# Rebuilding the two attentions of a two-layer kernel: paired maxima, single score banks, row sums inverted inside

## The reference

```python
x = L0_attn_x
xn = layernorm(x)
x = x + attn0(xn) + ternary_mlp(xn)      # attn0: 32 query heads of 16, 8 key heads, rope, causal softmax, wo
xn = layernorm(x)
x = x + gated_cumsum(xn) + attn1(xn)     # attn1: 16 heads of 32, causal softmax, Wp
# each attention: scores = q k^T * scale; softmax over the causal part; out = weight @ v; out @ w
```

## Time and profile before

| | |
|---|---|
| median of 3 runs | 3019.53 us (3016.12 to 3024.72) |
| profiled execution, its own time | 3012.14 us |
| its span | 3010.3 us |
| mean granted TensorE clock | 0.915 |
| TensorE busy (matmul) | 2623.4 us, 87% |
| VectorE busy | 1634.4 us, 54% |
| ScalarE busy | 1100.0 us, 37% |
| attention of layer 0 in the span, first load to last store | 554.1 to 1598.0 us |
| attention of layer 1, the same | 2155.8 to 2885.2 us |

### The profile page before, as it was taken

One profiled execution on the slowest core, in us unless ns is written; L12 is line 12 of the kernel. 1 busy time (PEld: TensorE's weight loads), 2 busy tenths in 40 slices (PEclk: granted clock), 3 DMA queues, 4 the chain that ended last, 5 costly groups with the idle time before them and its releaser, 6 DMA issues. The chain is left out here.

```text
span 3010.3 us, 38749 instructions
## 1 busy us (share of the span) xinstructions
PE 2623.4 (87%) x12386; PEld 1552.7 (52%) x12386; DVE 1634.4 (54%) x3332; ACT 1100.0 (37%) x1303; POOL 128.9 (4%) x84
## 2 busy tenths in 40 slices
PE   6969999589999999999995799797189999999945
PEld 3758888345555555555543577675144444444314
DVE  4644445587777777777712434311176665666313
ACT  2422222005565555555672222121014444444420
POOL 1200000300000000000000022100300000000000
PEclk8979999659999999999997899898569999999978
DMA  4741010401202202020003100252542122220023
GB/s 157 239 145 42 28 42 0 60 15 28 40 10 42 39 15 42 13 38 10 9 15 132 60 1 0 76 136 102 139 97 55 45 52 72 71 71 12 15 72 120
DMA packets 103924, 177.62 MB, mean 59 GB/s; under 512 B 39664, under 2 KB 45552, under 8 KB 97712
## 3 DMA queue, kind: packets, MB, share of 16 engines
q1 hardware_dynamic: 100272, 162.58, 20.7%
q10 hardware_dynamic: 3456, 12.58, 1.3%
HBM read 115.24 MB, written 59.90 MB: 58 GB/s over the span
## 5 line engine op out<-in xcount | busy, mean ns | idle before, releaser
L596 ACT ACTIVATE a_ex<-a_ps_s 128x1024 f32<-128x1024 f32 x960 | 832.6, 894 | 804.5 <-PE a_ps_s L668 404.1
L710 DVE TENSOR_REDUCE a_mx_part<-a_ps 128x1 f32<-128x512 f32 x1152 | 771.9, 688 | 255.0 <-PE a_ps L613 246.5
L613 PE MATMUL a_ps<-a_k,a_q 96*128 96x512 f32 (+3 forms) x1920 | 786.6, 452 | 97.4 <-DMA a_q<-q 92.8
L613 PEld LDWEIGHTS a_ps<-a_k,a_q 96*128 96x128 f32 x1920 | 369.5, 204 | 586.2 <-DVE a_mx_part L710 326.9
L635 PE MATMUL a_ps_o<-a_ex,a_v 128*32 128x512 f32 (+7 forms) x3840 | 607.6, 548 | 22.8 <-DVE a_o L735 19.1
L663 PE MATMUL a_ps_s<-a_q,a_k 128*128 128x512 f32 (+3 forms) x1920 | 607.6, 392 | 22.3 <-DMA a_q<-m_early 13.7
L706 DVE CUSTOM_DVE_ANT_0 a_junk<-a_ps,band 128x128 f32<-128x128 f32 (+3 forms) x768 | 369.3, 486 | 213.7 <-PE a_ps L613 210.5
L663 PEld LDWEIGHTS a_ps_s<-a_q,a_k 128*128 128x128 f32 x1920 | 353.4, 194 | 119.3 <-ACT a_ex L596 45.4
L635 PEld LDWEIGHTS a_ps_o<-a_ex,a_v 128*32 128x32 f32 (+1 forms) x3840 | 114.2, 117 | 212.9 <-issue 161.0
L668 PE MATMUL a_ps_s<-block_band,block_ident 128*128 128x128 bf16 x768 | 175.0, 234 | 0.0
L110 PE MATMUL w_ps<-w_oh,w_wh 128*128 128x512 f32 x128 | 54.7, 427 | 103.3 <-DVE w_ol L1042 103.3
(11 more groups left out here) (161 smaller groups left out, 2536.1 us busy)
## 6 DMA issues: line engine op xcount, KB each, us to landing
a_q<-q SPq DMA_DIRECT2D x48, 512.0 KB, 12.3
o<-a_o SPq DMA_DIRECT2D x64, 256.0 KB, 2.4
q<-p_oh SPq DMA_DIRECT2D x32, 256.0 KB
q<-p_ol SPq DMA_DIRECT2D x32, 256.0 KB
w_o<-o SPq DMA_DIRECT2D x32, 256.0 KB
w_z<-z SPq DMA_DIRECT2D x32, 256.0 KB
v<-p_v SPq DMA_DIRECT2D x32, 256.0 KB, 3.4
a_k<-k SPq DMA_DIRECT2D x8, 1024.0 KB, 8.4
```

What stands on the lines that cost most here:

```text
L596: act.activation(ex[unit % NE][:, :, off:CH], ps_s[unit % 2][:, :, off:CH], ACT.Exp, scale=SCALE).then_inc(exp_done, 1)
L613: pe.matmul(ps_1[bank][:, 0:w], q_st[set_][0:96, h, i * P:(i + 1) * P], k_st[set_][0:96, h % KH, kc * CH:kc * CH + w], start=True, stop=True)\
L710: dve.tensor_reduce(out, bank, AX.X, ALU.max).then_inc(taken1, 1)
```

## The change

What it does, part by part:

1. Pass 1 works on pairs of heads: two products into a pair of banks, and off the diagonal one VectorE reduction over both (128x2x512). Two pairs of banks take the place of three banks.
2. The score banks of pass 2 are three single ones, and exp works on one head at a time (1920 in place of 960). Six buffers `ex` instead of four.
3. Pass 1 runs `LEAD` = 21 steps ahead of pass 2 through all groups, not 40. Its rows are flipped per chunk, four times in a group.
4. The added mask product on the diagonal is f32r (`mask_sel`, `mask_low`, mask value -2^127), not bf16. Four constants are shaped on GpSimd one after another, two of them copied by DMA and all cast on VectorE before the first block ends.
5. The block `reciprocals` is gone. Inside the attention, SyncE reads the sums of each chunk back from DRAM (`load_sums`), VectorE inverts 128x16 or 128x8 of them (`invert`) and SyncE writes them (`store_sums`).
6. The chunk is copied out of PSUM by ScalarE (`stage`), not VectorE.
7. No loop: all groups are written out. No clearing of query and key tiles; the products take only the rows in use (48 or 96 in pass 1, 50 or 98 in pass 2), ones are set in 32 rows of the key tile.
8. `HALVES` is 1 for both attentions: all heads use rows from 0 on, and each head has a part of the query tile of its own.

The core of the diff, the new order of TensorE, SyncE and VectorE (constants, buffers and helpers that only change names are left out):

```diff
+LEAD = 21
+    FLIP_DELAY = 2 * PAIRS
+    FLIP_AT = {n + 1 + FLIP_DELAY: f for f, n in enumerate(sorted(LAST_BLOCK.values()))}
+    SLOTS = {s: range((s + LEAD) * PAIRS, (s + LEAD + 1) * PAIRS) for s in range(len(STEP_LIST))}
+    SLOTS[-1] = range(0, LEAD * PAIRS)
+    LAST_STEP = {s: (g, c) for s, (g, c, t) in enumerate(STEP_LIST) if t == TPC * c + TPC - 1}
...
         @block.sync
+            for g in range(2):
+                if ONES0 < KC:
+                    sp.wait_ge(blank, g + 1)
+                load(g)
+            for s in range(-1, len(STEP_LIST) + 8):
+                for n in SLOTS.get(s, ()):
+                    if n in FLIP_AT:
+                        put_rows(FLIP_AT[n], n)
+                if s >= 0 and s < len(STEP_LIST) and s % STEPS == 2 and s // STEPS + 2 < GROUPS:
+                    if s // STEPS > 0:
+                        sp.wait_ge(pv_done, s // STEPS * STEPS)
+                    elif ONES0 < KC:
+                        sp.wait_ge(blank, 3)
+                    load(s // STEPS + 2)
+                if s - 2 in LAST_STEP:
+                    store(*LAST_STEP[s - 2])
+                if s - 3 in LAST_STEP:
+                    load_sums(*LAST_STEP[s - 3])
+                if s - 6 in LAST_STEP:
+                    store_sums(*LAST_STEP[s - 6])
...
         @block.scalar
+            for s, (g, c, t) in enumerate(STEP_LIST):
+                if s - 2 in LAST_STEP:
+                    stage(*LAST_STEP[s - 2], s - 2)
+                for h in range(HG):
+                    act.wait_ge(scores2, n + 1)
+                    act.activation(ex[unit % NE][:, h % 2, off:CH], ps_s[n % 3][:, off:CH], ACT.Exp, scale=SCALE)\
+                        .then_inc(exp_done, 1)
...
         @block.tensor
+            for s, (g, c, t) in enumerate(STEP_LIST):
+                if t == 0:
+                    f = g * NCH + c
+                    pe.wait_ge(rows_in[f % 2], ROWS_IN * (f // 2 + 1))
+                for p in range(PAIRS):
+                    n = SLOTS[s][p]
+                    scores(s, 2 * p)
+                    if n in FLIP_AT:
+                        flip(n)
+                    if n < len(BLOCKS):
+                        max_scores(n)
+                    scores(s, 2 * p + 1)
+                if s > 0:
+                    times_v(s - 1)
...
         @block.vector
+            def invert(g, c):
+                j = g * NCH + c
+                dve.wait_ge(z_in[j % 2], 16 * (j // 2 + 1))
+                if j >= 2:
+                    dve.wait_ge(z_out[j % 2], 16 * (j // 2))
+                dve.reciprocal(zr[j % 2][:, :], z[j % 2][:, :]).then_inc(inverse, 1)
+            for s in range(-1, len(STEP_LIST) + 8):
+                for n in SLOTS.get(s, ()):
+                    if n in FLIP_AT:
+                        take_rows(n)
+                    if n < len(BLOCKS):
+                        maxima(n)
+                        g, i, kc, p = BLOCKS[n]
+                        if LAST_BLOCK[g, i // TPC] == n:
+                            whole_max(g, i // TPC, n)
+                if s - 5 in LAST_STEP:
+                    invert(*LAST_STEP[s - 5])
```

More of the change, by code:

```diff
@@ L443, in sem @@
         def sem(n):
[L445 to L451, removed]
+            return shared(f"at_{n}")
+        q_st = [sb(f"q{i}", [P, HG // HALVES, TOK], F32R) for i in range(NS)]
+        k_st = [sb(f"k{i}", [P, KH, TOK], F32R) for i in range(NS)]
+        v_st = [sb(f"v{i}", [P, VH, QT, VW]) for i in range(NS)]
@@ L452, in attention @@
         ex = [sb(f"ex{i}", [P, 2, CH]) for i in range(NE)]
         o_sb = [sb(f"o{i}", [P, CH]) for i in range(2)]
-        junk = [sb(f"junk{i}", [P, CH]) for i in range(NB)]
+        junk = [sb(f"junk{i}", [P, 2, CH]) for i in range(2)]
         mx_part = sb("mx_part", [P, HG, QT, NCH])
[L456 to L459, removed]
@@ L482, in attention @@
-        block = ctx.enter_context(nc.Block())
[L484 to L503, removed]
+        z_in = [sem(f"z_in{i}") for i in range(2)]
@@ L505, in _ @@
+        z_out = [sem(f"z_out{i}") for i in range(2)]
+        inverse = sem("inverse")
+        LOADS = (1 + 5 * HALVES) * 16
+        ROWS_IN = 16 * HALVES
+        block = ctx.enter_context(nc.Block())
         @block.sync
         def _(sp):
[L507 to L522, removed]
@@ L540, in store @@
-            def store(g, c):
[L541 to L565, removed]
@@ L568, in _ @@
             for b in range(2):
-                sp.wait_ge(stored[b], 16 * NCH // 2 * GROUPS + DMA0)
+                sp.wait_ge(stored[b], 16 * NCH * GROUPS // 2)
+                sp.wait_ge(z_out[b], 16 * NCH * GROUPS // 2)
         @block.gpsimd
         def _(pool):
[L573 to L580, removed]
+            for s in range(NS):
+                for e in range(HALVES):
+                    last = pool.memset(k_st[s][e * ROWS + ONES0:e * ROWS + ONES0 + 32].bitcast(F32), 1.0)
+                last.then_inc(blank, 1)
@@ L582, in _ @@
         @block.scalar
         def _(act):
[L584 to L590, removed]
-                    for pair in range(PAIRS):
-                        act.wait_ge(scores2, g * UNITS + unit + 1)
-                        if pair == 0:
-                            act.wait_ge(pv_done, g * STEPS + n + 1 - NE // PAIRS + PV0)
-                        act.activation(ex[unit % NE][:, :, off:CH], ps_s[unit % 2][:, :, off:CH], ACT.Exp,
-                                       scale=SCALE).then_inc(exp_done, 1)
-                        unit += 1
@@ L617, in flip @@
-            def flip(base, entry, count, early, first=False):
-                m = mx_early if early else mx_late
-                k = m.shape[1] * m.shape[2]
-                pe.wait_ge(part_max, count)
-                bank, before = bank1(entry, first)
-                pe.wait_ge(taken1, base + (before + 1))
-                pe.matmul(ps_1[bank][0:k, 0:P], m[:, :, :].rearrange("p h i -> p (h i)"),
+                if (i, kc, p) == (0, 0, 0):
+                    pe.wait_ge(landed[s], LOADS * (g // NS + 1))
@@ L712, in whole_max, with maxima @@
-            def whole_max(base, entry, early):
-                tiles = slice(0, EARLY_TILES) if early else slice(EARLY_TILES, QT)
-                dve.wait_ge(taken1, base + entry)
-                dve.tensor_reduce((mx_early if early else mx_late)[:, :, :], mx_part[:, :, tiles, :], AX.X, ALU.max)\
-                    .then_inc(part_max, 1)
-            def take_rows(base, entry, g, early, first=False):
-                n = 0 if early else 1
-                high, low = rows[early]
-                bank = ps_1[bank1(entry, first)[0]][0:high.shape[0], 0:P]
-                dve.wait_ge(scores1, base + (entry + 1))
-                if not isinstance(g, int) or g > 0 or not early:
-                    dve.wait_ge(rows_out[n], g * 32 + DMA0)
+            def maxima(n):
+                g, i, kc, p = BLOCKS[n]
+                m = entry(n)
+                w = min(CH, (i + 1) * P - kc * CH)
+                dve.wait_ge(scores1, m + 1)
+                bank = ps_1[m % 2]
+                if kc < i // TPC:
+                    dve.tensor_reduce(mx_part[:, 2 * p:2 * p + 2, i, kc], bank[:, :, 0:w], AX.X, ALU.max)\
+                        .then_inc(taken1, 1)
+                    return
+                for e in range(2):
+                    last = dve.tensor_tensor_reduce(out=junk[m % 2][:, e, 0:w], in0=bank[:, e, 0:w], in1=band[:, CH - w:CH],
+                                                    scale=1.0, scalar=NEG, op0=ALU.add, op1=ALU.max,
+                                                    accum_out=mx_part[:, 2 * p + e, i, kc:kc + 1])
+                last.then_inc(taken1, 1)
@@ new lines, in _ @@
+                pool.wait_ge(shaped, 3)
+                pool.affine_select(out=raw_low1[:, :], in_=raw_low1[:, :], compare_op=ALU.is_ge, fill=MASKED,
+                                   base=0, pattern=[[1, P]], channel_multiplier=-1).then_inc(shaped, 1)
+                pool.wait_ge(shaped, 4)
+                for part in range(2):
+                    pool.affine_select(out=raw_sel2[0:H, part, :], in_=raw_sel2[0:H, part, :], compare_op=ALU.not_equal,
+                                       fill=1.0, base=-1 - H * part, pattern=[[1, P]], channel_multiplier=-1)\
+                        .then_inc(shaped, 1)
+                    pool.wait_ge(shaped, 5 + part)
```

417 lines of the change are left out of this document (205 added, 212 removed).

## The result

The changed kernel took **3928.78 us** (median of 4 runs, 3926.66 to 3932.37) against 3021.23 for the kernel before, measured beside it: a ratio of 1.3007, 95% interval 1.2984 to 1.303. Forecast were 3086, with a range up to 3150. The sign was right. The size was not: some 840 us are missing from the sum, and no rival held them.

The account below looks back on a forecast made before the run. TensorE was taken to set the pace inside a group. Gains and costs summed to -89 us, the new wait added +155.5, so +66.5 on 3012.1, or 3086 us on the median; range 2985 to 3150.

Parts of the forecast that it names:

- the clearing at the start of layer 0: Layer 0's first load no longer waits for the clears, only one short memset is ahead of it: -8.8 us.
- the old 2.95 us per step: Layer 0's time per step with pass 1 beside pass 2, from the earlier profile: 117.9 us a group over 40 steps.
- The new wait: VectorE's inversion waits for sums read behind a load, stalling TensorE 10.0 and 13.6 us, five times per layer: +155.5 us.
- rival D: Chunk 3's rows, flipped in step 21, come late for step 24 in layer 1: 3096 to 3120 us, chance 0.10.
- rival A: The sums come in time, so the wait does not arise: 2930 us, faster than before, chance 0.20.
- rival B: The wait behind the load is there but half as long, +70 to +90: 3000 to 3020 us, chance 0.12.
- The sum without the wait: All priced parts of the change together, before the inversion's wait behind the load: -89 us.
- constants: Four more selects in a chain, a DMA and four casts before the first block: +5 us, bounds 3 and 8.
- wait for the copy-out: TensorE's 19.1 us of waiting for VectorE's copy in 42 places shrinks with ScalarE copying: -15 us, bounds 0 and -40.
- The term for the mask: Of 768 f32r mask products on the diagonal, 192 with 128 columns cost about 0.036 us more each: +7 us.
- The -2 for pairs of maxima: Pairing saves one of two VectorE reductions' start-up in 84 and 42 maxima of pass 1 alone: about -2 us.
- rival C: The f32r mask's weight loads are not hidden, +68 us on the forecast: 3150 us, chance 0.08.

Follow-up runs that it names:

- run 1: Changed kernel with layer 0's score products over many rows again (pass 1 96, pass 2 98) and the clearing back: 3061.14 us.
- run 2: Changed kernel with only a group's load moved from step 2 to step 30: 3849.85 us.
- run 3: Changed kernel with both edits, many rows in layer 0 and the load at step 30: 2924.04 us, 0.9674 of before.
- run 12: Kernel of run 3 with the mask product in bf16 instead of f32r: 2938.24 us.
- run 11: Changed kernel, load at step 30, split masks, layer 0's heads alternately on rows 0 to 49 and 64 to 113: 2894.64 us, 0.9568 of before.
- run 10: Changed kernel, load at step 30, each mask product split in two of 64 rows, all heads on rows 0 to 49: 3748.10 us.
- run 7: Kernel of run 3 with layer 0's pass 1 over 66 rows instead of 96, pass 2 still 98: 2947.02 us.
- run 8: Kernel of run 3 with layer 0's pass 1 over 64 rows instead of 96, pass 2 still 98: 3451.16 us.
- run 4: Kernel before the change with layer 0's pass 1 over 48 rows instead of 96, pass 2 still 128: 3370.26 us.
- run 9: Same kernel as run 8, run again four times: median 3455.29 us, spread 3330.32 to 3550.54.

## Why the prediction was wrong

**The step that failed is one that isn't there.** The prediction went through the change and took the clearing at the start of layer 0 as a gain of 8.8 us, but not what the clearing had been for. `KM` and the operands of pass 1 changed from 128 and 96 rows to 50 and 48 in layer 0, and the forecast carried the old 2.95 us per step over without a word. In the trace of before no product has fewer than 96 rows, so no row prices this. So a term of the sum was put at nothing without a reason. A bound was at hand: the earlier trace rows has a stretch with a clock of 0.57, and a layer at 0.50 throughout would have made seven groups of some 118 us more and a last one of 86, an estimate from the earlier trace rows of some 910. Run 1 puts the price of the rows at 868 us, and runs 2 and 3, without the wait behind the load, at 926. What the runs showed in place of the unchanged step is a granted clock of 0.50 through layer 0, 237 us a group, with TensorE busy all the time; why narrow products keep it there stays open.

**The sign was right in small part by the forecast's own mechanism.** With the rows put back (run 1) the kernel is 38 us slower than the one before beside it, which is the forecast's balance of gains and wait, and of the 908 us that were measured the rest is the rows'.

**The new wait: right, its size 13% too large.** Forecast +155.5; run 1 less run 3 gives 137. TensorE stood still for 105.0 us in ten waits, where the forecast had 5 x (10.0 + 13.6) = 118, and the other 32 are put down to the clock's fall (0.71 in run 1 between 772 and 782 us), where it had 37.5. No run shows that term by itself: it is five times 4.6 and 2.9 us, an estimate from what the loop's turn cost over a plain group, 7.6 and 5.9 us, less its gap of 3.0. The 2.9 in rival D is the same. Groups with a wait took 128 to 132 and 95.5 us, where 132 and 100 were forecast. In the changed kernel itself only layer 1's five were left (74 us by its groups, forecast 82.5), since the low clock hid the others. Rivals A and B fall with it: the sums do queue behind the load.

**The sum without the wait: -89 forecast, -86.6 measured** in the spans of before and run 3. By pieces:

| piece | forecast | measured |
|---|---|---|
| constants (first load 559.55 with the clearing kept, 554.12) | +5 | +5.4 |
| clearing gone (first load 550.58 in the change) | -8.8 | -9.0 |
| layer 0, first load to the last store of group 0 (243.1 to 192.7) | -52.2 and part of the copy | -50.4 |
| layer 0, groups 1 to 6 (714.9 to 701.8) | -7.6 and part of the copy | -13.1 |
| layer 0, last group (85.8 to 106.2) | +15.2 | +20.4 |
| layer 1, first load to the last store of group 0 (161.5 to 133.4) | -28.1 and part of the copy | -28.1 |
| layer 1, groups 1 to 6 (504.8 to 484.4) | -5.9 and part of the copy | -20.4 |
| layer 1, last group (63.2 to 70.9) | +9.5 | +7.7 |
| between the attentions and behind the second (no `reciprocals`) | -6 | -8.1 |
| wait for the copy-out (19.1 us), inside the rows above | -15 | 0.5 us left |

Run 3 keeps the clearing and so lacks the -8.8; without that term the forecast is -80, and run 3 did 6 us better. Most of that lies in layer 1's plain groups, 80.7 us each for 83.2, of which the forecast had only a part of the copy. The term for the mask, +7, was too high (no row shows its 0.036 us a product): the groups of run 12 give it about 2. The -2 for pairs of maxima was not tested by itself; one reduction over two heads takes 1225 ns in the change, two single ones took 2 x 688.

**Rivals C and D** did not happen: the mask's loads are hidden (run 12; C's +68 is their 75.1 us in the earlier trace rows less the 7 of the sum), and the changed kernel's scores of pass 2 wait 0.2 us in all for rows of maxima in the profile (L633 <-DMA a_q<-m).

## What to carry to other kernels

When an edit narrows the rows that a product contracts over, treat it as a change of speed and not of arithmetic. Zeros in the unused rows were free here (117.0 us a group with 96 rows, 116.9 with 66), and crossing from 66 to 64 rows cost some 500 us. Where few rows are wanted, put neighbouring products on different halves of the rows (run 11: 109.3 us a group for 223.5), keep those of one kind together (run 10: 223.5 for 237.0), and read the granted clock of the stage before anything else. A small read should not stand on the queue behind a large load when all that an engine does next stands behind its result: VectorE waited 13.8 us for it, and moving one number in the schedule was worth 137 us.

## What the runs showed of the hardware

- TensorE can be busy without a gap and keep half the clock to the end of a layer: with products of 48 and 50 rows on the same half (the change), the window of a whole group has 237.00 us busy of 237.00 at 0.50, and every other window of layer 0 has 0.50 too. With 96 and 98 rows (run 3) the first product of the layer starts at 578.67, the window from 578 to 640 us has 0.52, and every window from 640 us into the last group has 1.00.
- Which property of the narrow products keeps the level low is not settled. Run 10 (0.50) against run 11 (0.94) points at the use of one half only, since both have the same changes between the kinds (though run 11's last group fell to 0.50 all the same); run 7 against run 8 says that 66 rows, hardly more than 64, suffice (1.00 from 700 us on, with 64 rows from 1350). The two comparisons don't make one rule yet, and none is claimed. A kernel with pass 1 wide and pass 2 narrow, the missing fourth corner, was not tried.
- Products over 64 rows in turn with products over 98 cost 0.19 us more for each change at full clock than products over 66 in turn with 98: a pair follows a pair after 0.66 us in run 8, after 0.47 in run 7.
- Either level can hold for hundreds of microseconds in the same program (run 8: 0.50 from 640 to 1330 us, 1.00 from 1350 to 1900; run 4: 0.99 from 1300 to 1740). The time of run 9, the same kernel as run 8, spreads by 6%, where the others that were measured four times spread by 0.1% to 0.7%.
